# Attention with output projection in float32 pairs: the projection of each set of heads by seven block products instead of eight, its operands made within the attention

## The reference, cut

```python
xn = layernorm(x)                                   # x: (4, 512, 1024)
qkv = xn @ w_qkv                                    # 32 query heads, 8 key/value heads of 128
s = q @ k.T * 128**-0.5 - slope * sqrt(i - j)       # causal, per head
out = softmax(s) @ v                                # (4, 512, 4096)
y = x + out @ w_o + (xn @ W.T + b) + lora(xn)       # w_o: (4096, 1024); LoRA of routed rank, top 1
```

## Time and profile before

| | |
|---|---|
| time, median of 3 runs | 2568.79 us (2566.92 to 2569.37) |
| the profiled execution | 2571.17 us, its span 2569.4 us |
| granted clock, mean | 0.990 |
| PE busy | 2488.9 us, 97% |
| DVE (VectorE) busy | 1637.1 us, 64% |
| ACT (ScalarE) busy | 1025.1 us, 40% |
| POOL (GpSimd) busy | 176.0 us, 7% |
| chain that ended last | PE 91%, DVE 4%, ACT 2% |

### The profile page before, as it was taken

How to read it: one execution, slowest core, us unless ns; L and a number is a source line. 1 busy time by engine, 2 the same in 40 slices (tenths; PEclk the granted TensorE clock), 3 DMA queues, 4 the chain that set the end, 5 groups by cost and what they waited for, 6 DMA issues and landing times.

```text
span 2569.4 us, 32277 instructions
## 1 busy us (share of the span) xinstructions
PE 2488.9 (97%) x12512; PEld 2124.6 (83%) x12512; DVE 1637.1 (64%) x3305; ACT 1025.1 (40%) x2123; POOL 176.0 (7%) x230
## 2 busy tenths in 40 slices
PE   5999999996999999998899999999999999999998
PEld 4787888885778888887788888888888888888887
DVE  6657445555656455654866777677766777677763
ACT  4432133334533133333544444444444444444441
POOL 3211000001231000001000000000010000000000
PEclk8999999998999999999999999999999999999999
DMA  4536354464355435545632323232353233232311
GB/s 149 181 131 221 115 188 162 174 222 171 103 166 203 148 131 197 187 157 189 224 107 100 105 93 115 92 111 86 131 197 115 90 116 115 83 107 92 122 66 66
DMA packets 86489, 355.09 MB, mean 138 GB/s; under 512 B 8873, under 2 KB 9017, under 8 KB 77376
## 3 DMA queue, kind: packets, MB, share of 16 engines
q1 hardware_dynamic: 49680, 216.65, 24.3%
q0 software_dynamic: 36656, 136.38, 15.1%
HBM read 235.02 MB, written 117.97 MB: 137 GB/s over the span
## 4 chain that ended last, share of the span: by engine, by line
PE 91%; DVE 4%; ACT 2%; issue 1%; POOL 1%; DMA 1%; SPq 0%; DVEq 0%; ACTq 0%; POOLq 0%
PE ps L500 29%; PE ps L502 28%; PE ps L501 28%; PE ps L687 5%; DVE stats L958 1%; ACT rows L770 1%; ACT res_hi L741 1%; DVE w_lo L944 0%; DVE res_a L1034 0%; DVE res_a L944 0%; DVE res_b L1034 0%; ACT w_hi L741 0%; DVE res_b L944 0%; DMA rows<-x 0%; ACT probs L881 0%
## 5 line engine op out<-in xcount | busy, mean ns | idle before, releaser
L944 DVE TENSOR_TENSOR w_lo<-raw,w_hi 128x1024 fp32r<-128x1024 f32 x196 | 239.3, 1225 | 362.5 <-ACT w_hi L741 362.4
L500 PE MATMUL ps<-x_hi,w_hi 128*128 128x512 f32 x1120 | 436.7, 390 | 0.0
L502 PE MATMUL ps<-x_hi,w_lo 128*128 128x512 f32 x1120 | 436.3, 390 | 0.0
L501 PE MATMUL ps<-x_lo,w_hi 128*128 128x512 f32 x1120 | 436.2, 389 | 0.0
L741 ACT ACTIVATE w_hi<-raw 128x1024 fp32r<-128x1024 f32 x196 | 207.3, 1059 | 565.3 <-PE ps L502 445.1
L500 PE MATMUL ps<-wo_hi,at_hi 128*128 128x512 f32 x1024 | 412.1, 402 | 1.4 <-DVE at_lo L944 1.4
L502 PE MATMUL ps<-wo_hi,at_lo 128*128 128x512 f32 x1024 | 401.0, 392 | 0.0
L501 PE MATMUL ps<-wo_lo,at_hi 128*128 128x512 f32 x1024 | 398.7, 389 | 0.0
L881 ACT ACTIVATE probs<-probs,neg_max 128x512 f32<-128x512 f32 (+3 forms) x512 | 283.7, 565 | 193.9 <-DVE neg_max L1181 193.9
L1214 DVE TENSOR_TENSOR acc<-ps,acc 128x512 f32<-128x512 f32 x256 | 176.7, 690 | 164.1 <-issue 135.3
L741 ACT ACTIVATE at_hi<-ps 128x512 fp32r<-128x512 f32 x128 | 76.7, 599 | 509.2 <-PE ps L502 509.2
(11 more groups left out here) (147 smaller groups left out, 4051.7 us busy)
## 6 DMA issues: line engine op xcount, KB each, us to landing
raw<-w_all SPq DMA_DIRECT2D x70, 1024.0 KB, 5.3
q<-qk_s SPq DMA_DIRECT2D x128, 512.0 KB, 3.8
qk_s<-res_hi POOLq DMA_DIRECT2D x40, 1024.0 KB, 4.6
wo_raw<-w_o SPq DMA_DIRECT2D x64, 512.0 KB, 4.5
qk_s<-res_a POOLq DMA_DIRECT2D x20, 1024.0 KB, 9.1
qk_s<-res_b POOLq DMA_DIRECT2D x20, 1024.0 KB, 5.3
k<-qk_s SPq DMA_DIRECT2D x32, 512.0 KB, 3.6
v<-v_s SPq DMA_DIRECT2D x32, 512.0 KB, 5.7
```

The lines of the kernel that those rows point to most:

```text
L500: pe.matmul(to, st_hi, mv_hi, start=start, stop=False, skip_group_check=True)
L501: pe.matmul(to, st_hi, mv_lo, start=False, stop=False, skip_group_check=True)
L502: return pe.matmul(to, st_lo, mv_hi, start=False, stop=stop, skip_group_check=True)
L944: nc.vector.tensor_tensor(to, source, high.bitcast(F32), ALU.subtract).then_inc(signal, 1)
```

## The change

A set's four heads are 512 rows of w_o. The product of the set's output (512 tokens x 512) with those rows (512 x 1024) is cut in 2x2 blocks: tokens in halves (tile t with tile t+2), heads in pairs, columns in halves of 512. For each of two tile pairs, seven products of sums of blocks replace eight of blocks. Products 0, 1 and 3 start a bank; the others add onto the bank of two products before, and after every product VectorE adds the bank to one block of acc.

- ScalarE copies a head's output whole (`at_raw`) and later makes the high parts of the seven left operands (`out_high`, 128x256 each, 14 a set) and of the seven right ones (`out_split`, 128x1024, seven per two sets). It also does `normalise`, four activations with the reciprocal as scale; VectorE keeps the reciprocal.
- GpSimd makes the sums (`out_sum`, eight of 128x256 a set; `wo_sums`, four of 128x1024 per two sets) and the low parts of the left operands (`out_low`, 14 a set). VectorE makes the low parts of the right operands and the 14 adds a set.
- The right operands have one buffer (`wo`): the splits of the next group go in where the products of the group before have been used, at the ends of units 3, 4 and 5 of eight. `wo_raw` is loaded as four blocks by SyncE's queue, which also gets the loads and stores of acc from GpSimd's queue.

```diff
+SHARES = (range(0, 4), range(4, 7), range(7, 11), range(11, 14))
+OUT_SUMS = ((0, 3), (1, 3), (0, 2), (0, 6), (0, 4), (1, 2), (1, 6), (1, 4))
+OUT_SPLITS = ((), (0, 1), (2, 3, 4), (5, 6))
+WO_SUMS_IN = ((4,), (2,), (3, 5), ())
...
         def fills(n):
             s, c = (n - 1) // G - 1, (n - 1) % G
...
-            part = tiles_of(s)[2 * c:2 * c + 2]
-            return [(s, tt, half, 8 * s + 2 * c + i) for i, (tt, half) in enumerate(part)]
+            return [(s, part // STEPS, part % STEPS) for part in SHARES[c]]
+        def shaped(n):
+            s, c = n // G - 1, n % G
+            if c == 0:
+                return ([], [(s, 0)]) if 0 <= s < SETS else ([], [])
...
+            return {1: ([(s, 1), (s, 2), (s, 3)], [(s, 4), (s, 5), (s, 6)]),
+                    2: ([], [(s, i) for i in range(7, 11)]),
+                    3: ([], [(s, i) for i in range(11, 14)])}[c]
+        def making(n):
+            group, since = (n - 2) // (2 * G), (n - 2) % (2 * G)
+            return (group, since) if n >= 2 and group < GROUPS and since < G else (None, None)
+        def used(group, step):
+            return PARTS * (2 * group - 1) + STEPS + step + 1
...
@@ sync
+                if n in range(3, 7):
...
+                    for tt in ((0, 2), (1, 3), (4, 6), (5, 7))[n - 3]:
+                        sp.dma_start(acc[:, tt, :], acc_s[bass.ds(tt * P, P), :]).then_inc(s_acc_in[tt], 16)
+                if n % (2 * G) == G + 3 and group + 1 < GROUPS:
+                    sp.wait_ge(s_wo_lo, STEPS * (group + 1))
+                    sp.wait_ge(s_wo_sum, len(WO_SUMS) * (group + 1))
+                    for i in range(4):
+                        out_block(group + 1, i)
...
+            for t in range(2 * QT):
+                sp.wait_ge(s_acc, PARTS * (SETS - 2 + t // QT) + (STEPS if t % 2 == 0 else PARTS))
+                store_out(PAIRS - 1, t // QT, t % QT)
@@ gpsimd
+            def out_low(s, part):
+                if s:
+                    pool.wait_ge(s_fill, PARTS * (s - 1) + part + 1)
+                pool.wait_ge(s_op_hi, PARTS * s + part + 1)
+                nc.gpsimd.tensor_tensor(op_lo[:, part], op_source(s, part), op_hi[:, part].bitcast(F32),
+                                        ALU.subtract).then_inc(s_op_lo, 1)
+            def wo_sums(group, step):
...
+                if step in (2, 3) and group:
+                    pool.wait_ge(s_fill, used(group, step))
...
+                if step == 5:
+                    pool.wait_ge(s_wo_lo, STEPS * group + 2)
+                nc.gpsimd.tensor_tensor(to, first, second, op).then_inc(s_wo_sum, 1)
+            for n in range(UNITS + G + 1):
+                at_once, later = shaped(n)
+                s, c = n // G - 1, n % G
+                for group, step in out_sums_in(n) if c == 0 else ():
+                    wo_sums(group, step)
+                if c == 0 and at_once + later:
+                    pool.wait_ge(s_at_raw, G * s + 2)
+                    for tile, k in OUT_SUMS[0:2]:
+                        out_sum(s, tile, k)
+                if at_once:
+                    pool.wait_ge(s_at_raw, G * (s + 1))
+                    for tile, k in OUT_SUMS[2:4]:
+                        out_sum(s, tile, k)
+                for part in at_once:
+                    out_low(*part)
...
@@ tensor
+            def fill_in(s, tile, k):
...
+                pe.wait_ge(s_op_lo, f + 1)
                 if f >= 2:
                     pe.wait_ge(s_acc, f - 1)
...
+                for kt in range(2):
+                    cols = slice(kt * 512, (kt + 1) * 512)
+                    last = product(fill[f % 2][:, :], (op_hi[:, part, kt, :], op_lo[:, part, kt, :]),
+                                   (wo[:, k, 0, cols], wo[:, k, 1, cols]), kt == 0 and k in STARTS, kt == 1)
...
+                todo = fills(n)
+                for f in todo[:1]:
+                    fill_in(*f)
                 if 1 <= n <= UNITS:
                     transposes(n - 1)
-                for f in fills(n):
+                for f in todo[1:3]:
                     fill_in(*f)
                 if 1 <= n <= UNITS:
                     attend(n - 1)
+                for f in todo[3:]:
+                    fill_in(*f)
@@ scalar, iteration n
+                if 2 <= n < UNITS + 2:
                     outputs(n - 2)
+                for part in at_once:
+                    out_high(*part)
                 if 1 <= n < UNITS:
                     exponential(n, 0)
                 if 1 <= n <= UNITS:
                     transposed(n - 1)
+                if 1 <= n < UNITS:
+                    for c in range(1, QT):
+                        exponential(n, c)
+                for part in later:
+                    out_high(*part)
                 if n < UNITS:
...
+                    normalise(n)
+                for part in out_splits(n):
+                    out_split(*part)
@@ vector, iteration n
-                if 2 <= n < UNITS + 2:
-                    outputs(n - 2)
                 if 1 <= n < UNITS:
                     maxima(n)
+                for f in todo[:1]:
+                    add_fill(*f)
                 if 1 <= n <= UNITS:
                     transposed(n - 1)
-                todo = fills(n)
-                for f in todo[:1]:
-                    add_fill(*f)
                 if n < UNITS:
-                    normalise(n)
-                    if chunk_in(n) is not None:
-                        out_weights(chunk_in(n))
+                    inverses(n)
                 for f in todo[1:]:
                     add_fill(*f)
+                for part in out_splits(n):
+                    out_split(*part)
```

More of the change, by code:

```diff
@@ L109, in block_program @@
         v = at("v", 16 * K, [P, 2, 2, SEQ], F32R)
-        wo_raw = at("wo_raw", 24 * K, [P, 2, HIDDEN])
+        wo_raw = [at(f"wo_raw{i}", (24, 28, 42, 46)[i] * K, [P, 1024]) for i in range(4)]
+        at_raw = [[at(f"at_raw{i}{j}", ((160, 164), (168, 50))[i][j] * K, [P, 2, SEQ]) for j in range(2)] for i in range(2)]
         dist = at("dist", 32 * K, [P, SEQ])
@@ L276, in unit @@
             return pr, g, b, h
-        def tiles_of(s):
-            b = unit(s * G)[2]
-            return [(b * QT + t, half) for t in range(QT) for half in range(2)]
         def fills(n):
@@ new lines, in _ @@
+            for n in range(UNITS + G + 1):
[13 more added lines that the diff above has]
+                    out_low(*part)
+                if at_once:
+                    out_sum(s, *OUT_SUMS[4])
+                if c == 2 and later:
+                    for tile, k in OUT_SUMS[5:8]:
+                        out_sum(s, tile, k)
+                for part in later:
+                    out_low(*part)
+                for group, step in out_sums_in(n) if c != 0 else ():
+                    wo_sums(group, step)
@@ L1187, in maxima, with inverses @@
                     bias_of((g + 1) % KV_HEADS, h)
-            def normalise(n):
+            def inverses(n):
                 dve.wait_ge(s_exp, QT * (n + 1))
+                if n:
+                    dve.wait_ge(s_probs, n)
                 nc.vector.reciprocal(row_inv[:, :], row_sum[:, :]).then_inc(s_inv, 1)
-                dve.wait_ge(s_inv, n + 1)
-                for i in range(QT):
-                    tile = probs[:, n % 2, OFF[i]:OFF[i] + (i + 1) * P]
-                    last = nc.vector.tensor_scalar(tile, tile, row_inv[:, i:i + 1], None, ALU.mult)
-                last.then_inc(s_probs, 1)
             def transposed(n):
```

224 lines of the change are left out of this document (144 added, 80 removed).

## The result

The changed kernel takes 2589.61 us (median of 4 runs, 2589.15 to 2591.4) against 2567.86 (median of 4, 2566.77 to 2569.37) for the one before on the same chip. The ratio is 1.0086, with a 95% interval of 1.0068 to 1.0103: slower, by about 22 us. The forecast was 2547, with a range of 2512 to 2590. The measured time lies at the very end of that range, and on the other side of "no change" than the forecast.

The account below looks back on a forecast made before the run. TensorE was taken to bound the kernel, busy 97% of the span. Terms -87.0 (matmuls), +61.5 (group stalls) and +3 (start and end) sum to -22.5; from 2571.2, less 2.4 to the median, 2547 us, range 2512 to 2590.

Parts of the forecast that it names:

- The matmuls: Output projection on TensorE: 384 fewer matmuls, all on the path, at 0.2266 us each, -87.0 us.
- The averages: Attention stretch, per unit: ScalarE 8.15 us, VectorE 6.6, GpSimd 5.1; none full on average, so the whole 87 us is gained.
- The forecast's other estimate: GpSimd's 128x1024 sum: 2.35 us from a documented 2048-column time, beside the 2.38 used.
- its two lows to 3.6 if they go through together: Unit 4 of eight: VectorE makes both weight lows by 3.6 us, attend at 8.5 instead of 7.1, 1.4 us lost.
- rival A: Unit 4: the port changes hands after each instruction; 3.85 us lost, 6.55 a group, 2583 us; chance 0.34.
- Units 5 and 6: Units of eight with late splits and lows: 2.4 us lost in unit 5, 0.3 in unit 6.
- the sum: Losses of units 4, 5 and 6 together: 4.1 us in eight units, +61.5 us over fifteen groups.
- that assumption: Unit 4: VectorE's two weight lows go through together, without GpSimd's sum between them.
- Rival C: Units 4 and 5: TensorE's clock falls to 1.2 GHz, 1 to 2 us per group; 0.10 including ordinary units not fitting.
- A with C: Port turns after each instruction plus the clock's fall in each group: 2600 us or over.
- Start and end: First group's splits add +3 us (0 to 8); the tail's +2 is counted inside the start's rounding.

Follow-up runs that it names:

- the third experiment: Changed kernel with w_o's operands made for the first group only, later loads, sums, splits and lows left out: 2488.4 us (one run).
- first experiment: Changed kernel with GpSimd's four sums of weights 32 columns wide instead of 1024 from the second group on: 2549.0 us (one run).
- fifth: Changed kernel with GpSimd's two first small sums of unit 4 ahead of the weights' sums of steps 3 and 5: 2571.5 us (one run).
- the second experiment: Changed kernel with VectorE's lows of weights as one-source copies with an accumulator, subtraction left out: 2544.9 us (one run).
- the ninth experiment: The eighth with splits 2, 2, 3, small sums first, and unit 4's output copy ahead of normalise: 2525.48 us (4 runs).
- the eighth: The fourth, plus GpSimd's step 2 sum waiting for the group's first two lows and the bias product behind adds: 2533.07 us (4 runs).
- the fourth: Changed kernel with ScalarE's weight splits ahead of normalise and VectorE's lows before the fourth add: 2553.43 us (4 runs).
- the sixth: Changed kernel with 26 unread 128x128 matmuls on TensorE in the wait of unit 4: 2596.9 us (one run).

## Why the prediction was wrong

**The matmuls, right.** 2688 of them, and -87.0 us: the third experiment has 77.81 us for eight units where before had 83.15, and ordinary units of 9.03 and 10.42 against the 9.0 and 10.36 forecast.

**The averages, right in kind.** Window 1280 to 2440 of the changed kernel, at 10.60 us a unit 109.4 units: ScalarE 857.41/109.4 = 7.84 us a unit (8.15 forecast), GpSimd 5.35 (5.1), VectorE 7.35 (6.6; the waits at the port count as busy there: the lows of raw blocks average 1759 ns over 1260 to 2540 where 1221 was their length, the bias product 702 instead of 487). GpSimd's 128x256 lows take 0.74 to 0.75 us where 0.71 was forecast, the large sums 2.35 to 2.42 where 2.38 was. The forecast's other estimate, 2.35, was worked out from the 4497 ns for 2048 columns in the Trainium skill's "GPSIMD Engine Reference", section "Performance versus the Vector engine", and the row at 512; the trace agrees. The four normalisations on ScalarE take 715, 608, 501 and 398 ns, less 0.1 each 1.82 us a unit, where 1.83 was forecast.

**The failed step: unit 4, "its two lows to 3.6 if they go through together".** They don't. The port passes to the engine that waits, after each instruction, even between two VectorE instructions that stand back to back in its queue. The second low ended at 5.7 us, the add at 9.1. Where the clock stayed up the unit lost 12.69 - 9.03 = 3.66 us instead of 1.4, which is rival A's 3.85; in the mean it lost 14.11 - 9.03 = 5.08, and the 1.4 more is the clock, which unit 5 gives back. The forecast had the reading that would have told it, GpSimd's second operation that was already begun and still lost its turn, and weighed it at 0.34 because VectorE never had two such instructions in a row. That was an absence of evidence, not evidence against: no row showed an engine keeping the port.

**Units 5 and 6.** Forecast 2.4 and 0.3; the means are 0.98 and 0.82, and unit 7 has 0.08. The 0.98 looks like a miss and isn't: where the clock stays up, unit 5 loses 12.79 - 10.42 = 2.37 us, with unit 4 at 12.69, at 9.59 (first experiment) or at 11.47 (fifth). The two losses add, and the fall of the clock in unit 4 hides most of the second. The path is the forecast one too. In a group without a fall, whose unit 5 starts at 1756.47, ScalarE's third split ends 2.8 us in (3.0 forecast), GpSimd's two sums are held up by the third low, and the first product's low part is there 6.55 us in (6.8 forecast):
```profile
1759.82 2.52 POOL L586 TENSOR_TENSOR op_raw<-at_raw,op_raw 128x256 f32<-128x256 f32 x2 [5.01 <-ACT at_raw L892]
1762.30 0.72 POOL L592 TENSOR_TENSOR op_lo<-at_raw,op_hi 128x256 fp32r<-128x256 f32 x1
```
Unit 6 is a term that was sized too small: 0.88 us without a fall instead of 0.3. So of the 6.97 - 4.1 = 2.9 us a group that the forecast missed, 2.3 are unit 4's turns and 0.6 are unit 6.

**The nearest test of the sum with that assumption made true** is the second experiment: units 4, 5 and 6 lose 1.55, 1.87 and 0.55, together 4.0 us a group where 4.1 was forecast, and the kernel takes 2544.9 us where 2547 was. It frees a little more than was assumed, since its lows never wait (they end 3.2 us into unit 4, not 3.6), and the bias product waits longer than was counted (1.59 us); the add that TensorE needs ends at 7.1 us, where the forecast had 7.0. That the sums agree within 0.1 us is in part luck: unit 5 is 0.5 less than forecast, units 4 and 6 0.15 and 0.25 more.

**The clock.** Rival C's fall happens, for 3.41 or 6.83 us in 13 of the 15 groups, and costs the changed kernel some 0.5 us in all. C had added 1 to 2 us for each fall; it left out that unit 5 had a stall of its own to take it up. A with C was priced at 2600 or over; it is 2590.

**Start and end, small.** Spans differ by 18.0 us: -87.0 for the matmuls, +104.6 for 15 groups of 6.97, and +0.4 left. The scores of unit 1 come 3.2 us earlier (1214.9 instead of 1218.06). Unit 0 is 1.4 us shorter in every kernel with the change (15.6 instead of 17.0); the rest lies in the first stage, which is the same in all, and in the kernels with the change unit 1 starts anywhere from 1214.0 to 1217.8. The 8th unit starts between 1277.1 and 1285.8 over all these kernels. The seven units from there take 66.0 us instead of 63.7, on the side of the +3 forecast. The stores of acc now land in 4.7 us at the median instead of the 2.9 of the earlier trace rows, and nothing in the end waits longer for it.

**The ledger** of the 22 us between the medians is so: a forecast of -22.5, plus 15 x (6.97 - 4.1) = 43 more in the groups, less 2.6 at start and end (+0.4 for the +3), makes +18.0, the spans' difference; the rest is the spread of single runs.

## What to carry to other kernels

- In these kernels two engines that share a port exclude each other by the instruction. Price a critical VectorE instruction at its own length plus the longest GpSimd instruction that may be waiting, once for each instruction in a row, until a trace shows that a queue keeps the port.
- Work that nobody needs soon is not free when it holds what others need. A semaphore wait that keeps it out of the way (here 17 us for one) can be worth more than moving the critical work, which took the meeting with it.
- When a stall is mended, look at the next unit before counting the gain, and sort the groups by whether the clock fell before comparing means. Here the clock alone made unit 5 look 1.4 us better in the changed kernel, and the ninth experiment 0.4 us a group better than the eighth.
- Try the rate with the suspected work left out first, as the third experiment does; it tells how much there is to win.

## What the hardware showed that was not expected

- GpSimd and VectorE take turns also when one of them has its next instruction ready: two lows 4.84 us around one sum of 3.18, three lows 5.13 us with small sums between.
- VectorE's `tensor_scalar` with one SBUF tensor waits as well: the bias product takes 1.10 and 2.57 us instead of 0.49, the normalisation 837 ns on average instead of 481. The form with an accumulator doesn't: 1207 to 1220 ns over 80.
- Behind the same 3.3 us of idle time TensorE's clock fell to 1.2 GHz in 12 of 14 groups and stayed at 2.4 in two. The fall began between 0.8 us before TensorE resumed work and 1.3 us after, and lasted 3.41 us in nine groups and 6.83 in three.
- The same fall can cost nothing or about 1 us. One of 3.4 us cost 0.0 in the changed and the fifth kernel, where a later stall took it up, and 0.9 to 1.3 us in the fourth, the sixth and the eighth, where little or nothing did. With 26 matmuls in the wait of unit 4 it came in unit 5 of six groups instead.
